# A decoder layer stack on one core: new orders for VectorE, ScalarE and GpSimd in the third stage

## The reference

```python
for i in range(DEPTH):                                    # 6 layers, 16 heads of 64
    x = attn_layer(shift_tokens(x), Wqkv[i], q_scale[i], k_scale[i], Wo[i]) + x
    x = ffn_layer(shift_tokens(x), ln_g[i], ln_b[i], W1[i], b1[i], W2[i], b2[i]) + x

# attn_layer: q, k, v = x @ Wqkv by heads
q = l2norm(q) * qs;  k = l2norm(k) * ksc
q = q * cos * scale + rotate_half(q) * sin * scale        # rotary products
k = k * cos / scale + rotate_half(k) * sin / scale
sim = q k^T * 8, masked (causal, window 32);  attn = softmax(sim);  out = (attn v) @ Wo

# ffn_layer
xn = (x - mu) / sqrt(var + 1e-5) * g + bln
a, gate = split(xn @ W1 + b1);  return a * gelu(gate) @ W2 + b2
```

## Time and profile before

| | us |
|---|---|
| median of 3 runs | 3696.78 |
| lowest and highest | 3694.6, 3710.01 |
| the profiled execution, time | 3706.61 |
| its span in the profile | 3704.8 |
| PE busy | 3253.5 (88%) |
| DVE busy | 2801.0 (76%) |
| POOL busy | 2652.6 (72%) |
| ACT busy | 2487.4 (67%) |

### The profile page before, as it was taken

How to read it: one execution, slowest core, us unless ns; L and a number is a source line. 1 busy time by engine, 2 the same in 40 slices (tenths; PEclk the granted TensorE clock), 3 DMA queues, 4 the chain that set the end, 5 groups by cost and what they waited for, 6 DMA issues and landing times.

```text
span 3704.8 us, 124977 instructions
## 1 busy us (share of the span) xinstructions
PE 3253.5 (88%) x51333; PEld 2530.0 (68%) x51333; DVE 2801.0 (76%) x5681; ACT 2487.4 (67%) x4952; POOL 2652.6 (72%) x5005
## 2 busy tenths in 40 slices
PE   8999997888888888888888888888888888888886
PEld 6778775666666666666666666766666666666665
DVE  6844446888787888887888878788778878888885
ACT  5756664676666767666667667677666766667664
POOL 5522227877787887787778877777777778777774
PEclk9999999999999999999999999999999999999999
DMA  4000004444445444444444444444444444444442
GB/s 96 3 8 8 8 6 96 102 95 94 87 103 109 92 93 90 100 104 97 94 93 89 101 104 97 90 93 95 103 103 94 95 88 98 94 98 90 97 95 52
DMA packets 280546, 310.50 MB, mean 84 GB/s; under 512 B 154281, under 2 KB 225582, under 8 KB 279982
## 3 DMA queue, kind: packets, MB, share of 16 engines
q0 software_dynamic: 58368, 201.36, 28.0%
q1 hardware_dynamic: 220892, 100.93, 10.7%
q10 hardware_dynamic: 722, 0.21, 0.0%
HBM read 23.63 MB, written 2.10 MB: 7 GB/s over the span
## 4 chain that ended last, share of the span: by engine, by line
PE 59%; DVE 25%; issue 8%; ACT 5%; POOL 1%; SPq 1%; DMA 1%; DVEq 0%; POOLq 0%
PE bank L1153 10%; PE bank L1235 8%; PE bank L1209 8%; PE bank L1123 8%; DVE RK L1403 6%; DVE Z L1459 6%; PE bank L1094 6%; DVE ss L1424 6%; PE bank L1110 4%; PE bank L1134 3%; ACT sq L1300 3%; ACT xnT L1283 2%; PE bank L709 2%; PE bank L722 2%; PE bank L731 2%
## 5 line engine op out<-in xcount | busy, mean ns | idle before, releaser
L1403 DVE TENSOR_TENSOR RK<-bank,tables 128x1024 f32<-128x1024 f32 x384 | 468.7, 1222 | 329.3 <-ACT sq L1300 326.2
L1209 PE MATMUL bank<-xnT,W 128*128 128x128 f32 (+1 forms) x2304 | 322.8, 294 | 350.0 <-DVE Y L1376 349.3
L1389 DVE TENSOR_TENSOR RQ<-bank,q_tables 128x1024 f32<-128x1024 f32 x384 | 452.1, 1219 | 153.3 <-ACT sq L1294 153.2
L1209 PEld LDWEIGHTS bank<-xnT,W 128*128 128x128 f32 (+1 forms) x2304 | 282.6, 190 | 371.0 <-issue 371.0
L1546 POOL TENSOR_TENSOR P<-P,inv_sum 128x512 f32<-128x512 f32 x384 | 505.7, 1634 | 5.7 <-DVE inv_sum L1471 5.7
L1534 POOL TENSOR_TENSOR RK<-RK,rn 128x512 f32<-128x512 f32 x384 | 400.2, 1042 | 28.4 <-POOL rn L1574 0.9
L1520 POOL DMA_DIRECT2D RQ<-RQ x384 | 350.1, 1041 | 97.2 <-DVE RQ L1389 90.2
L1153 PE MATMUL bank<-WA,xcT 128*128 128x512 f32 x768 | 376.8, 613 | 37.0 <-DVE P L1450 16.7
L1540 POOL TENSOR_TENSOR P<-P,rn 128x512 f32<-128x512 f32 x384 | 402.4, 1048 | 3.8 <-DVE P L1450 3.8
L1267 ACT ACTIVATE kT<-bank 128x512 f32<-128x512 f32 x384 | 229.5, 598 | 249.8 <-PE bank L1094 249.8
L1235 PE MATMUL bank<-WO,OT 128*128 128x128 f32 x3072 | 382.3, 278 | 0.0
(11 more groups left out here) (166 smaller groups left out, 7567.4 us busy)
## 6 DMA issues: line engine op xcount, KB each, us to landing
RQ<-RQ POOLq DMA_DIRECT2D x384, 256.0 KB, 4.0
RK<-RK POOLq DMA_DIRECT2D x192, 512.0 KB, 4.7
Z<-Z SPq DMA_DIRECT2D x768, 64.0 KB, 2.5
WA<-in_wqkv SPq DMA_DIRECT2D x24, 256.0 KB, 2.8
ystat<-Y SPq DMA_DIRECT2D x192, 32.0 KB
ystat<-Y SPq DMA_DIRECT2D x384, 15.8 KB
ys<-Y SPq DMA_DIRECT2D x192, 32.0 KB
ys<-Y SPq DMA_DIRECT2D x384, 15.8 KB
```

The source lines that it names most:

```text
L1209: last = mm(FF_BANK[c][0:rows, side * 128:(side + 1) * 128], m.W1[:, off + at:off + at + rows], m.xnT[:, t % 2, :], start=True, stop=True)
L1389: tt(both, src.unsqueeze(1).to_broadcast([128, 2, 8, SEQ]), m.q_tables[:, layer(t), :, :].unsqueeze(2).to_broadcast([128, 2, 8, SEQ]), ALU ...
L1403: tt(both, src.unsqueeze(1).to_broadcast([128, 2, 16, 32]), tab.unsqueeze(2).to_broadcast([128, 2, 16, 32]), ALU.mult).then_inc(s.rotated. ...
```

## The change

Only the third stage is touched. On VectorE `ff_added(i - 8)` stands directly behind `statistics(i - 5)`, the two key rotary products change places, both maxima are together, the second transpose stands behind them, and the subtractions, row sums, `gated` and inverses follow in a new order. On ScalarE both key halves are squared before xnT is copied, and copies and exponentials are re-ordered. On GpSimd `keys_added` and `inverse_deviation` go forward and `queries_added` goes behind the second scaling of the probabilities. The counts of `rotated`, `less` and `row_sum` follow the new orders, and three waits are added for buffers and banks that the old order had covered. TensorE's and SyncE's lists of steps are untouched. Lines of the new kernel are two to three higher than those of the old from L1150 on.

```diff
-    s.qk, s.squared, s.rotated = counted("qk", *four), counted("squared", (QUERIES, 0), (QUERIES, 1), (KEYS, 1), (KEYS, 0)), counted("rotated", *four)
+    s.qk, s.squared, s.rotated = counted("qk", *four), counted("squared", (QUERIES, 0), (QUERIES, 1), (KEYS, 1), (KEYS, 0)), counted("rotated", (QUERIES, 0), (QUERIES, 1), (KEYS, 1), (KEYS, 0))
...
-    s.scores, s.mx, s.less = sem("local_scores"), counted("mx", 0, 1), counted("less", 0, 1)
-    s.scaled, s.probs, s.row_sum = counted("scaled", 0, 1), counted("probs", 1, 0), counted("row_sum", 0, 1)
+    s.scores, s.mx, s.less = sem("local_scores"), counted("mx", 0, 1), counted("less", 1, 0)
+    s.scaled, s.probs, s.row_sum = counted("scaled", 0, 1), counted("probs", 1, 0), counted("row_sum", 1, 0)
...
                     at_least(pe, s.less.sem, s.less.upto(1, t - 1))
+                else:
+                    at_least(pe, s.h, 3 * (t - 7))
...
-                if j == 1 and t == N - 1:
-                    pe.wait_ge(s.y1, t - 3)
+                if j == 1:
+                    at_least(pe, s.y1, t - 3)
...
-            keys_out(i - 1, 1)
             squares(i, KEYS, 1)
             if i == 0:
                 m.cross_tail()
+            keys_out(i - 1, 1)
             query_lengths_out(i)
-            normal_out(i - 6)
             squares(i, KEYS, 0)
             keys_out(i - 1, 0)
+            normal_out(i - 6)
+            exponents(i - 2, 1)
             values_out(i, 1)
-            exponents(i - 2, 1)
             outputs_out(i - 4, 1)
+            values_out(i, 0)
             outputs_out(i - 4, 0)
-            values_out(i, 0)
             exponents(i - 2, 0)
...
-                if half == 0:
+                if half == 1:
                     at_least(dve, s.k_turned.sem, s.k_turned.upto(0, t))
...
                 dve.wait_ge(s.mx.sem, s.mx.upto(a, t + 1))
+                at_least(dve, s.p_turned.sem, s.p_turned.upto(a, t - 1))
...
             statistics(i - 5)
+            ff_added(i - 8)
+            key_rotary(i, 1)
+            query_floor(i)
             key_rotary(i, 0)
-            query_floor(i)
-            key_rotary(i, 1)
             squares_summed(i)
             probs_turned(i - 3, 1)
-            probs_turned(i - 3, 0)
-            ff_added(i - 8)
             seeded(i)
             maximum(i - 1, 0)
-            row_sums(i - 2, 0)
+            maximum(i - 1, 1)
+            probs_turned(i - 3, 0)
+            less_maximum(i - 1, 1)
             less_maximum(i - 1, 0)
             row_sums(i - 2, 1)
-            maximum(i - 1, 1)
             attention_added(i - 4)
+            row_sums(i - 2, 0)
+            gated(i - 7)
             inverse_sums(i - 2, 1)
-            gated(i - 7)
-            less_maximum(i - 1, 1)
             inverse_sums(i - 2, 0)
...
-                pool.wait_ge(s.rotated.sem, s.rotated.upto((KEYS, 1), t + 1))
+                pool.wait_ge(s.rotated.sem, s.rotated.upto((KEYS, 0), t + 1))
...
         for i in range(N + LAST + 1):
+            probs_scaled(i - 3, 1)
+            inverse_deviation(i - 5)
+            keys_added(i)
+            probs_scaled(i - 3, 0)
             queries_added(i)
-            probs_scaled(i - 3, 1)
-            probs_scaled(i - 3, 0)
-            keys_added(i)
-            inverse_deviation(i - 5)
             inverse_lengths(i)
```

## The result

The changed kernel takes 3865.13 us (median of 4 runs, 3854.42 to 3869.3); the kernel before took 3699.64 (median of 4 runs, 3694.6 to 3710.01). The ratio is 1.0439, with a 95% interval from 1.0407 to 1.0472. The change makes the kernel 4.4% slower. The forecast was 3710, with a range up to 3810, so the time lies above the range.

The account below looks back on a forecast made before the run. A loop through VectorE and SyncE was to replace the old cycle: 7.06 + 0.04 + 7.15 + 1.90 = 16.15 us a tile, unchanged; 3697 plus 13 us for held-up tiles gave 3710 us, range 3620 to 3810.

Parts of the forecast that it names:

- The mechanism: Third stage: the wait before L1209 goes; a loop of statistics, VectorE, SyncE's ten issues and landing binds at 16.15 us.
- The third rival: Loop over SyncE not closed or not binding, so the whole wait before L1209 goes: 3347 us, chance 0.08.
- The two waits on TensorE: Added for keys' second half on `h` and keys' turn on `y1`; claimed to cost nothing.
- VectorE's part: From the start of the statistics to the end of the second transpose on VectorE: 7.06 us a tile.
- the hand-over: From the end of the second transpose on VectorE to SyncE's first Z issue: 0.04 us.
- SyncE's stretch: From SyncE's first Z issue to its last `ys` issue: 7.15 us, against 6.39 undisturbed.
- The first rival: SyncE's stretch stays between 6.39 and some 6.9 us, Z served between RQ's packets: most likely 3633 us, chance 0.20.
- The landing: From SyncE's last `ys` issue to the start of VectorE's next statistics: 1.90 us with stragglers.
- the allowance of 0.07: 0.07 us a tile for tiles where the queue is held up longer; 13 us over some 187 tiles.
- The second rival: SyncE's queue held up longer, every fourth tile paying 1.73 us, 0.43 a tile: 3790 us, chance 0.22.

Follow-up runs that it names:

- `ys` first: The three `ys` loads issued ahead of the three `ystat` loads on SyncE: 3453.98 us on the changed kernel, 3691.78 us on the kernel before.
- the scaling early: Changed kernel with GpSimd's second scaling of the probabilities directly behind the first, ahead of the additions' DMAs: 3828.7 us, ratio 1.0345.
- RQ first: Changed kernel with `queries_added` (the two accumulating RQ DMAs) at the top of GpSimd's iteration: 3906.29 us, ratio 1.0551.

## Why the prediction was wrong

**The mechanism** held at each step that it names. The wait at L1209 went (5.1 us are left), TensorE waits before the mask products instead, the statistics wait in each of the 142 tiles between 1000 and 3400 us (454.7 us, 3.2 each), and one loop through VectorE and SyncE sets the time. Two experiments show it: `ys` first gives 411 us after the change and 9 before. The third rival (3347, no loop over SyncE) is excluded by the same.

**The two waits on TensorE,** costed at nothing: one is not quite. The keys' products (L1155) wait 72.3 us for H, the gated product of VectorE. They stand outside the loop, and TensorE waits for the loop anyway, so nothing in the sum fails by it.

**VectorE's part, 7.06 us with 0.04 for the hand-over:** here the sum failed. It measured 7.74. The 0.49 for the three seed instructions came from a place in the old order where GpSimd ran nothing long beside them. In the new order the first of them falls into GpSimd's scaling and takes 0.72 instead of 0.15, and the three take 1.06 from start to start (2005.85 to 2006.91). That is 0.57 of the 0.64 us. The prediction had that scaling in its own layout of GpSimd's queue, right behind RK's issue, but asked only when the DMAs would go out, not what it does to VectorE. The experiment with the scaling early shows this cause. The Trainium skill has the rule, "SBUF — State Buffer", section Who interferes with whom: VectorE's `tensor_scalar` can enter a mode that needs the port pair shared with GpSimd, whichever of the two comes first holds it for its whole instruction, and the other is blocked. The trace agrees: L1433 ends at 2006.57, the scaling at 2006.52. So it is in all 160 tiles between 800 and 3500 us: L1433 ends 0.03 to 0.05 us behind the scaling. In 6 of them it is held for about 1.75 us.

**SyncE's stretch, 7.15 us:** measured 7.11, but the agreement is in part luck. The prediction took 7.15 from tiles in which RK came late, with 3.0 us of filled DMA engines behind the first Z issue. In the trace of before the stretch is already 7.0 us or more in 59 of the 155 tiles where RK isn't late, issued some 2.06 us ahead of the first Z (mean 6.80), so the five late tiles by themselves don't show a price of being late. And the engines were filled for some 2.4 us behind the first Z issue and not 3.0, since that issue came 0.58 us later behind the statistics than in the prediction, at 2008.83. Stretches of the changed kernel (granted clock, DMA share and GB/s last):

```profile
2008.60:2011.20 2.60, 2.60 (x26) 2.60 (x25) 2.60 (x6) 2.42 (x5) 1.94 (x9) 1.00 1.04 202
2011.20:2014.00 2.80, 2.80 (x16) 1.80 (x16) 1.92 (x7) 2.47 (x5) 2.49 (x5) 1.00 0.41 108
```

With the scaling early RK goes out 3.83 us ahead of the first Z, nearly the prediction's 3.76, and there the stretch is 7.45. So, as an estimate, a right VectorE's part would have come with a stretch of some 7.45 and not 7.15. What held is that RQ lengthens the stretch: with RQ first its median is 6.40 us, against 7.05 in the changed kernel. The first rival (3633) is excluded: the second Z issue is held, 1.28 us in the median instead of 0.67.

It was the case for which I had cited the Trainium skill, "DMA: Bandwidth & Descriptors", section Queues, rings and completion order, by which each DMA engine goes round-robin between its queues, packet by packet. The measured stretch decides against what I had made of that rule, a stretch that stays short; it doesn't test the rule itself.

**The landing, 1.90:** the mean is 2.08, the median 1.89. The difference is 23 stragglers among 158 tiles, 2.80 to 3.93 us.

**The sum:** 7.74 + 7.11 + 2.08 = 16.93 us, against 16.22 with the allowance of 0.07. Of the 0.71 in between, 0.64 is VectorE's part, 0.18 the landing, -0.04 the stretch and -0.07 the allowance for a queue that is held up longer. Times 187 it is 133 us; with the forecast's 3710 that is 3843, 11 us under the profiled run (3854.42), the fastest of the four, and 22 under their median. Most of the 11 comes from counting on from 3697, the median of the kernel before: the rows are of an execution that took 3706.61, and 3706.61 with 0.78 more a tile for 187 tiles is 3852.5.

**The second rival** (3790, the queue held longer) is not what happened, although its time is nearer: no mean stretch of 7.6 and more is in the trace of the changed kernel.

**The range** was drawn round the wrong term. Both of its ends came from SyncE's stretch. VectorE's part, 7.06 us of instructions that had all been measured somewhere else, had no bounds at all. Had L1433 been bounded above by the rest of a GpSimd instruction (some 1.3 us instead of 0.15, for 187 tiles), the upper end would have been above 3900, an estimate.

**What stays open.** Why single `ys` landings take up to 3.93 us with no RQ near was not tried; with `ys` first only 3 of 177 are above 2.4 us. Nor was it tried how long SyncE's issues would be with RK's transfer away, since no order here has it elsewhere.

## What to carry to other kernels

When a wait is removed from a software pipeline, close every loop of one iteration and compare their lengths, queues of DMA issues included: here three of them lay between 15.6 and 16.9 us, and the order that took the other two away made the third the bound, until three loads changed places on the queue. A duration goes with its neighbour: an instruction moved beside another engine's instruction needs a bound for that pair and not the row of its old place. A transfer that fills the DMA engines cost time here both beside the loop's DMA issues and beside its landing, so before moving it, ask what part of the loop it will lie beside.

## What the runs showed of the hardware

- A VectorE instruction on 128x16 numbers took 0.719 us (median) when started inside GpSimd's 128x512 scaling, ended 0.03 to 0.05 us behind it in 160 tiles, and took 0.195 with the scaling moved. The longest took 1.776.
- The issue of a DMA on SyncE is not of fixed length. While accumulating DMAs of GpSimd filled the DMA engines (share 1.04), the second of four Z issues took 1.28 us in the median (0.84 to 1.99) instead of 0.67, and the stretch of ten issues grew from 7.11 to 7.90 us as the first came nearer to RK's issue (4.35 to 2.81 us).
- The landing of three small `ys` loads went from 1.89 to 4.12 us when 512 KB of RQ were issued 0.23 us ahead of the last of them; the median was 3.22 us over 96 tiles with RQ ahead, and 1.89 over 61 with RQ behind.
- After a wait of 3.00 us TensorE's granted clock was 0.57 over the 4 us in which the next products began (2002 to 2006), and twelve products took 2.90 us; after a wait of 1.83 us the clock was 1.00 and they took 1.57. In the changed kernel, where TensorE waits 264.7 us before the mask products in 137 tiles between 1000 and 3400 us, the clock was 0.972 over the execution (0.986 before). These products stand outside the loop: VectorE waited for TensorE in only 14 of those tiles, 11.9 us in all.
